# One rotary stage of a transformer layer's front moved from GpSimd to VectorE

## The reference

```python
qg = hidden_states @ Wq                      # queries and gate
k, v = hidden_states @ Wk, hidden_states @ Wv
q, k = rope(q), rope(k)                      # x_rot * cos + rot * sin, on 16 of 64 dimensions
scores = einsum('bkgsd,bktd->bkgst', q, k) / sqrt(64)
attn = softmax(scores)
out = einsum('bkgst,bktd->bkgsd', attn, v) * silu(gate)
x = layernorm(x + out @ Wo)
x = layernorm(x + ffn(x))                    # ternary w_fc, w_proj, low-rank term, relu squared
```

## Time and profile before

| | us |
|---|---|
| median of 3 runs | 1775.32 (1773.26 to 1776.89) |
| the profiled execution | 1773.95 |
| its span (first to last instruction) | 1772.1 |
| busy in the span: PE, DVE, POOL, ACT | 1674.5, 1378.8, 1030.5, 710.5 |

### The profile page before, as it was taken

The page is one execution under the profiler, slowest core; times in us unless marked ns, Lnnn a source line. Parts: engine busy times, 40 slices in busy tenths (PEclk is TensorE's granted clock), DMA queues, the critical chain, the costliest instruction groups (busy, mean ns, idle before and its releaser), DMA issues.

```text
span 1772.1 us, 24588 instructions
## 1 busy us (share of the span) xinstructions
PE 1674.5 (94%) x6902; PEld 858.6 (48%) x6902; DVE 1378.8 (78%) x1692; ACT 710.5 (40%) x895; POOL 1030.5 (58%) x765
## 2 busy tenths in 40 slices
PE   5699999999999999999878999999999999999996
PEld 3444444444444444447744444444444444444685
DVE  6678888878887787757767778888888888886587
ACT  1234444444444443444332444444444444444352
POOL 0556666666666665654344666666666666657342
PEclk9789999999999999999887999999999999999998
DMA  4600001111111100020043000010000000000001
GB/s 163 160 14 23 23 23 25 24 26 27 27 24 24 25 20 1 1 77 25 25 115 82 23 23 23 23 24 23 22 22 23 22 22 22 19 1 1 24 25 48
DMA packets 36906, 59.68 MB, mean 34 GB/s; under 512 B 6624, under 2 KB 17264, under 8 KB 36288
## 3 DMA queue, kind: packets, MB, share of 16 engines
q1 hardware_dynamic: 36800, 58.50, 12.6%
HBM read 20.07 MB, written 4.19 MB: 14 GB/s over the span
## 4 chain that ended last, share of the span: by engine, by line
PE 75%; DVE 12%; issue 7%; POOL 3%; DMA 2%; ACT 1%; SPq 0%; DVEq 0%; POOLq 0%; ACTq 0%
PE ob L568 23%; PE sc L553 14%; PE sc L556 11%; PE mx L526 11%; PE misc L506 6%; PE mx L665 3%; DVE acc L323 2%; DVE maxp L1040 2%; POOL acc L323 2%; PE misc L579 1%; DVE maxp L1178 1%; PE sc L632 1%; PE ob L680 1%; DMA acc<-in_x 1%; DVE oge L1069 1%
## 5 line engine op out<-in xcount | busy, mean ns | idle before, releaser
L323 POOL TENSOR_TENSOR acc<-acc,probs 128x512 f32<-128x512 f32 x448 | 602.8, 1346 | 365.8 <-DVE acc L323 353.4
L1040 DVE TENSOR_REDUCE maxp<-mx 128x2 f32<-128x1024 f32 x468 | 567.1, 1212 | 232.3 <-PE mx L528 225.8
L820 ACT ACTIVATE probs<-sc 128x1024 f32<-128x1024 f32 x512 | 501.2, 1025 | 574.5 <-PE sc L556 574.5
L568 PE MATMUL ob<-probs,v_sb 128*64 128x512 f32 x2048 | 496.3, 605 | 0.5 <-ACT probs L820 0.5
L323 DVE TENSOR_TENSOR acc<-acc,probs 128x512 f32<-128x512 f32 x448 | 422.8, 944 | 23.5 <-ACT probs L820 22.6
L553 PE MATMUL sc<-qa,kab 128*128 128x512 f32 x1024 | 351.1, 424 | 0.0
L556 PE MATMUL sc<-qb,kab 128*128 128x512 f32 x1024 | 320.8, 394 | 0.0
L526 PE MATMUL mx<-kab,qa 64*128 64x512 f32 x490 | 248.4, 507 | 32.3 <-DMA kab<-high_sb 12.4
L528 PE MATMUL mx<-kab,qa 64*128 64x512 f32 x490 | 247.9, 506 | 0.0
L526 PEld LDWEIGHTS mx<-kab,qa 64*128 64x128 f32 x490 | 91.1, 186 | 295.3 <-issue 153.1
L568 PEld LDWEIGHTS ob<-probs,v_sb 128*64 128x64 f32 x2048 | 124.0, 136 | 212.6 <-issue 149.7
(11 more groups left out here) (130 smaller groups left out, 1549.0 us busy)
## 6 DMA issues: line engine op xcount, KB each, us to landing
qa<-high_sb SPq DMA_DIRECT2D x128, 128.0 KB, 2.3
qb<-low_sb SPq DMA_DIRECT2D x64, 128.0 KB, 2.3
tables_sb<-in_tables SPq DMA_DIRECT2D x34, 128.0 KB, 2.4
xT_sb<-in_xT SPq DMA_DIRECT2D x2, 2048.0 KB, 9.4
acc<-in_x SPq DMA_DIRECT2D x8, 512.0 KB, 4.1
out_y<-acc SPq DMA_DIRECT2D x8, 512.0 KB, 3.2
kab<-acc SPq DMA_DIRECT2D x24, 128.0 KB, 2.4
rot_sb<-raw_sb SPq DMA_DIRECT2D x72, 32.0 KB, 1.8
```

The source lines that it names most:

```text
L323: ops.tensor_tensor(total, total, part, ALU.add).then_inc(summed, 1)
L568: mm = nc.tensor.matmul(ob[hd * D:(hd + 1) * D, :], v_sb[:, t, kv * D:(kv + 1) * D], probs[:, k % RING, hd * CHUNK:(hd + 1) * CHUNK], star ...
L820: nc.scalar.activation(probs[:, k % RING, :].rearrange("p (h n) -> p h n", h=2), sc[:, 2 * (k % 2):2 * (k % 2) + 2, :], ACT.Exp, scale=flo ...
L1040: nc.vector.tensor_reduce(two_columns(p, j), mx[:, :, :], AX_X, ALU.max).then_inc(maxed, 1)
```

## The change

Stage 3 (the third key chunk) is marked as DVE's instead of POOL's, so POOL's loop leaves it out. DVE does stages 0 and 1 as before, the first two maxima of the first key chunk, then stage 3, and goes on with the maxima. No other engine's program changes.

```diff
-        FRONT = [("q", 0, 0, "dve"), ("k", 0, 1, "dve"), ("k", 1, 2, "pool"), ("k", 2, 3, "pool"),
+        FRONT = [("q", 0, 0, "dve"), ("k", 0, 1, "dve"), ("k", 1, 2, "pool"), ("k", 2, 3, "dve"),
                  ("k", 3, 0, "pool"), ("q", 1, 1, "pool"), ("q", 2, 0, "pool")]
...
-                for s in range(PRO):
-                    if FRONT[s][3] == "dve":
-                        rope(nc.vector, front(s), b)
-                        rope_add(nc.vector, front(s), b)
-                        if FRONT[s][2] >= 2:
-                            dve.wait_ge(y_stored, 16 * (NCH * b + 1))
-                        rope_low(nc.vector, front(s), b)
+                def front_rope(s):
+                    rope(nc.vector, front(s), b)
+                    rope_add(nc.vector, front(s), b)
+                    if FRONT[s][2] >= 2:
+                        dve.wait_ge(y_stored, 16 * (NCH * b + 1))
+                    rope_low(nc.vector, front(s), b)
+
+                front_rope(0)
+                front_rope(1)
                 for i in range(PASSES):
                     front_reduce(0, i)
+                    if i == TILES // 2 - 1:
+                        front_rope(3)
                 final_max(b, 0, 0)
```

## The result

| | us |
|---|---|
| kernel before, median of 7 runs | 1777.15 (1773.26 to 1779.46) |
| changed kernel, median of 7 runs | 1784.71 (1782.69 to 1788.38) |
| changed to before | 1.0046, 95% interval 1.0034 to 1.0059 |
| profiled execution of the changed kernel, and its span | 1784.71, 1782.8 |

The changed kernel is slower by 0.46%, about 8.2 us (6.0 to 10.5) by this ratio. The forecast was +5.1 us: the sign is right, the size is not. The two profiled executions differ by 10.7 us of span, but the one of before lies 3.2 us under the median of its seven runs and the one of after on its own median, so the pair shows some 3 us more than the medians do.

The account below looks back on a forecast made before the run. The prediction took TensorE, busy 94% of 1772.1 us, to bound the kernel. Delays of 2.9 and 2.2 us in the two fronts gave +5.1 us, median 1775.32 to 1780.4 us; range 1776.8 to 1784.8, rounded.

Parts of the forecast that it names:

- The chain through the sixth maximum: Each batch's front: the sixth row maximum frees pass 7's bank; v_group(3) and stage 6 queue behind pass 7 on PE.
- the formula for the loss: Sixth maximum's delay: time DVE is held less 2.42 us (first batch, 2.9 us) or 3.14 us (second, 2.2 us).
- The collisions: Stage 3 on DVE meets POOL's stage 4: two products wait 0.65 and 1.2 us, so DVE is held 5.3 us.
- What POOL saves is worth nothing: POOL starts stage 4 about 2.1 us earlier, but only waits longer for ACT before stage 5: path gain nothing.
- the fronts' sum: Delay of the sixth maximum in both batches' fronts together: 2.9 + 2.2 = +5.1 us.
- The clock at nothing: TensorE's clock over v_group(3), stage 6 and the first scores: changes put at 0 in the forecast.
- rival 2: v_group(3) and stage 6 run at 1.2 GHz in one or both batches: 1782.6 to 1784.8 us, chance 0.14.
- the ends that were kept for the range: Clock effects on v_group(3), stage 6 and first scores: per batch +2.2 us, or -4.8 us.
- the sum itself: Whole kernel: 2.9 + 2.2 = +5.1 us for the two batches, taking the median from 1775.32 to 1780.4 us.

## Why the prediction was right about the direction and wrong about the size

1. *The chain through the sixth maximum* was right, and so was the formula for the loss (time held less 2.42 us, less 3.14 us). In the changed kernel it gives 5.15 - 2.42 = 2.73 and 4.62 - 3.14 = 1.48; the traces show 2.72 and 1.48 between first and sixth maximum. The changed kernel with six memsets (held 5.15 and 4.91 us), the place behind the fourth maximum and the wait on POOL follow it to 0.03 us. The 2.42 us, though, belong to the one profile that was read: there v_group(2) ran in part at the upper clock in the first batch (0.58 on average, 64.20 to 67.40) and the gap was short. In the five other profiles without stage 3 among the maxima the sixth maximum stands 8.80 to 8.83 us behind the first in both batches, as in the second batch before (8.82). Against these the changed kernel (10.83 and 10.30) loses 2.0 and 1.5 us, 3.5 in all.
2. *The collisions* were right in kind: the order of the two engines is as worked out, POOL from 61.15 (61.5 forecast). DVE was held 5.15 and 4.62 us where 5.3 was put; in the second batch the first product met less of POOL. So the fronts' sum in this pair of profiles was 4.2 us and not 5.1. The rule of the Trainium skill ("SBUF — State Buffer", section "Who interferes with whom") that the prediction cites agrees with these numbers, reductions included: the maxima took 1.20 to 1.23 us with POOL at work and without.
3. *What POOL saves is worth nothing*: right; its wait for ACT grew from 4.52 to 8.33 us.
4. *The clock at nothing*: in this pair of profiles it wasn't. v_group(3) ran at 0.50 in the first batch, against 0.60 before, and the pair with stage 6 took 6.09 us (73.41 to 79.50) instead of 4.94:

```profile
73.41:76.98 3.57, 3.57 (x18) 3.57 (x17) 1.48 (x2) 0.00 (x0) 0.00 (x0) 0.50 0.91 202
```

   That is half of what rival 2 has for one batch. The first scores gave 1.0 us back there (5.73 us from the first to the weighted values, 95.02 to 100.75, against 6.72), and took 1.2 more in the second batch (6.86, 962.82 to 969.68, against 5.70 from 957.35 to 963.05). Together +1.3 us, inside the ends that were kept for the range. One pair of profiles can't say whether the change did this. Over all profiles the pair of v_group(3) and stage 6 plus the first scores take 11.8 us on average in the eight fronts with stage 3 among the maxima (10.3 to 12.4), and 10.9 in the twelve without (10.3 to 11.7; this kind includes the kernel before). That speaks for some 0.9 us a batch which the prediction put at nothing, but the ranges overlap and no run tests it.
5. *The step that failed* is the sum itself: it had terms for the two fronts only. The cost of the added instructions was counted where they run, and what they do to the place of the attention loop in VectorE's program was put at nothing; it was not even named among the things moved. It measures 3.45 us by the steps at the four jumps, in the changed kernel and in the one that has nothing but ten idle instructions more, and with six idle instructions more in the changed kernel it goes. The fronts' term of 5.1 us came out near: 3.5 to 4.2 us for the maxima, and perhaps 1 to 2 for the clock.

The account of the profiled pair is then 4.2 (maxima) + 1.3 (clock) + 3.45 (jumps) = 9.0 of 10.7 us. Of what remains, 2.3 us lie behind the last attention unit (8.4 us at its copy, 10.7 at the end), less 0.4 us ahead of each front's first maximum. These are not explained; the profiled pair differs by 3 us more than the medians, so they may be scatter. By ratios, the fronts are worth 0.0033 (changed kernel less the one with stage 3 early) and the stops 0.0024 (less the one with six memsets), together 0.0057 against 0.0046 measured at once: consistent within the intervals, but no sharper.

## What to carry to other kernels

A step that is moved to another engine is free only if it fits in that engine's waits ahead of the work that others stand in line for; here the wait of 6.5 us before the first maximum held it, the place behind the second did not. Instructions added ahead of a hot loop also move the loop in its engine's program: look at the first instructions behind each jump for idle time that the profile puts down to nothing, and try a few idle instructions in the setup before judging a change by a few tenths of a per cent. When two engines hold each other up, letting the one that has time wait can be the faster order.

## What the runs showed of the hardware that was not expected

- Behind a backward jump of VectorE's loop the first instruction came 0.52 to 0.90 us after the last one's end when the loop began at 146, 151 or 156 of the program, and with no idle time at 162. With the loop at 156 there was a second stop two instructions on (0.86 us at 305.81). At 146 and 151 no second stop is seen; a border at the same number would lie twelve and seven instructions behind the loop's first.
- The Trainium skill ("Runtime: NRT & Kernel Launch", section "Instruction fetch mechanics") says that an engine streams its program in pages of 256 instructions, holds two of them, and waits for a fetch when a jump's target lies outside these. The runs agree with it if the two pages held at the jump (numbers 434 to 450) are the one in which the jump stands and the one before it: a border at 158 and the next 256 further, at 414, would leave the targets 146, 151 and 156 outside, and 162 inside. That the stop is a fetch of instructions was not measured on its own, and the border's number was fitted to the stop. Shown is that the stops go with the place of the loop: the kernel before and the changed one, brought to the same place (156 or 162), show the same.
